# Who makes the low halves of the last four weight groups, and from which copy

## The reference

```python
x = x + layernorm(attn_ref(layernorm(x), ...))       # in_proj, conv, selective scan, gate, out_proj
x = x + layernorm(ffn_ref(layernorm(x), ...))

def ffn_ref(input, SU_ug, SU_dp, Wscale_ug, Wscale_dp, W_up, W_gate, W_down):
    x = fwht(x * SU_ug) / SCALE
    x_up = x @ W_up.T * (Wscale_ug[:INTER] * SCALE)
    x_gate = x @ W_gate.T * (Wscale_ug[INTER:] * SCALE)
    x = silu(x_gate) * x_up
    x = fwht(x * SU_dp) / SCALE
    return x @ W_down.T * (Wscale_dp * SCALE)
```

## Time and profile before

| | us |
|---|---|
| median of 3 runs | 2675.09 (2675.07 to 2676.07) |
| the profiled execution | 2677.31 |
| its span, first to last instruction | 2675.5 |
| PE busy | 2581.3 (96%) |
| DVE busy | 2238.6 (84%) |
| POOL busy | 2046.8 (77%) |
| ACT busy | 1818.1 (68%) |

### The profile page before, as it was taken

The page is one execution under the profiler, slowest core; times in us unless marked ns, Lnnn a source line. Parts: engine busy times, 40 slices in busy tenths (PEclk is TensorE's granted clock), DMA queues, the critical chain, the costliest instruction groups (busy, mean ns, idle before and its releaser), DMA issues.

```text
span 2675.5 us, 46296 instructions
## 1 busy us (share of the span) xinstructions
PE 2581.3 (96%) x16048; PEld 2190.1 (82%) x16048; DVE 2238.6 (84%) x2567; ACT 1818.1 (68%) x3939; POOL 2046.8 (77%) x1692
## 2 busy tenths in 40 slices
PE   7899889999999999999999999999999999989998
PEld 6566568989888898989888898988888898978887
DVE  6698799898889889898889889888889889989421
ACT  4576677777777767777777767777777767755322
POOL 6576778788797978888797988888797988777222
PEclk9999999999999999999999999999999999989999
DMA  5554245666666665766666665666666665656674
GB/s 179 193 185 151 105 164 199 232 214 219 227 217 218 217 228 198 242 211 228 228 213 217 216 227 204 237 210 235 217 219 219 212 220 205 228 177 233 259 269 164
DMA packets 165193, 564.41 MB, mean 211 GB/s; under 512 B 17248, under 2 KB 19680, under 8 KB 132960
## 3 DMA queue, kind: packets, MB, share of 16 engines
q1 hardware_dynamic: 164960, 561.44, 60.7%
HBM read 527.30 MB, written 34.08 MB: 210 GB/s over the span
## 4 chain that ended last, share of the span: by engine, by line
PE 77%; DVE 10%; ACT 8%; issue 3%; DMA 1%; POOL 1%; SPq 0%; POOLq 0%; DVEq 0%; ACTq 0%
PE pF L717 21%; PE hT L624 14%; PE pM L642 13%; PE pD L733 10%; PE pM L694 8%; DVE h L1147 5%; DVE acc L1160 3%; PE pD L754 3%; PE pM L664 3%; PE decay L717 2%; ACT decay L968 1%; PE hT L616 1%; PE pF L754 1%; ACT delta L945 1%; ACT delta L940 1%
## 5 line engine op out<-in xcount | busy, mean ns | idle before, releaser
L1147 DVE TENSOR_TENSOR_SCAN h<-decay,dbx 128x512 f32<-128x512 f32 x1024 | 1200.7, 1206 | 97.8 <-ACT decay L968 68.2
L1315 POOL TENSOR_TENSOR dbx<-u,bb 128x2048 f32<-128x2048 f32 (+1 forms) x272 | 1179.1, 4336 | 37.7 <-DVE h L1147 35.7
L968 ACT ACTIVATE decay<-delta,a_neg 128x255 f32<-128x255 f32 x2048 | 875.5, 468 | 310.0 <-DVE h L1147 302.6
L1160 DVE SCALAR_TENSOR_TENSOR acc<-hT,bcT,acc 128x1024 f32<-128x1024 f32 x480 | 609.3, 1269 | 127.7 <-PE hT L624 124.3
L717 PE MATMUL pF<-fxT_hi,wug 128*128 128x256 f32 x3632 | 710.2, 289 | 0.4 <-issue 0.4
L624 PEld LDWEIGHTS hT<-ident,h 128*128 128x128 f32 x4096 | 472.8, 141 | 148.5 <-issue 96.7
L717 PEld LDWEIGHTS pF<-fxT_hi,wug 128*128 128x128 f32 x3632 | 583.6, 192 | 0.9 <-issue 0.8
L624 PE MATMUL hT<-ident,h 128*128 128x128 f32 x4096 | 535.2, 274 | 33.6 <-DVE acc L1160 22.5
L717 PE MATMUL pF<-fxT_lo,wug 128*128 128x256 f32 x1816 | 514.8, 283 | 0.0
L642 PE MATMUL pM<-xnT,w_in 128*128 128x256 f32 x2016 | 480.9, 382 | 10.4 <-ACT hid L888 4.7
L642 PEld LDWEIGHTS pM<-xnT,w_in 128*128 128x128 f32 x2016 | 367.2, 192 | 55.8 <-ACT hid L888 6.3
(11 more groups left out here) (166 smaller groups left out, 2788.9 us busy)
## 6 DMA issues: line engine op xcount, KB each, us to landing
wug<-scratch_ug SPq DMA_DIRECT2D x243, 1024.0 KB, 4.8
wd<-scratch_wd SPq DMA_DIRECT2D x243, 512.0 KB, 4.0
w_in<-in_W_in SPq DMA_DIRECT2D x252, 256.0 KB, 2.9
bb<-scratch_bc SPq DMA_DIRECT2D x128, 256.0 KB, 4.7
xb<-in_hidden_states SPq DMA_DIRECT2D x16, 512.0 KB, 5.0
xr<-in_hidden_states SPq DMA_DIRECT2D x16, 512.0 KB, 5.9
out<-xr SPq DMA_DIRECT2D x16, 512.0 KB, 3.5
kept_ug<-scratch_ug SPq DMA_DIRECT2D x7, 1024.0 KB, 7.6
```

Source lines behind the costliest of these rows:

```text
L968: e = act.activation(da[q % 2][:, i, 1:], delta[c % 2][:, dt, 1:], ACT.Exp, scale=a_neg[:, dt, n:n + 1])
L1147: dve.tensor_tensor_scan(row(h[n % 2][:, tiles, :]), row(da[q % 2][:, :, :]), row(dbx[n % 2][:, tiles, :]), 0.0, ALU.mult, ALU.add).then_i ...
L1160: dve.scalar_tensor_tensor(acc[c % 2][:, tb, :], hT[:, :], cn, acc[c % 2][:, tb, :], ALU.mult, ALU.add).then_inc(acc_done, 1)
L1315: pool.tensor_tensor(dbx[n % 2][:, tiles, :], u[:, tiles, :], rows, ALU.mult).then_inc(done if restarts(c) else prod_done, 1)
```

## The change

For tiles 32 to 47 ScalarE reads the bank twice: after the high half it writes the same scaled tile again, unrounded, to one of two rows of `xr[1]`, which holds nothing else at that time. POOL, which makes no use of PSUM here, subtracts the high half from that copy and so makes the low half; VectorE no longer touches these tiles. TensorE now waits for the copy (`had_raw`) before it uses a bank again. POOL's 16 subtractions stand behind its `dbx` product of the even slot two or three after the one where ACT evacuates. Tiles 0 to 31 stay as they were.

```diff
+        FIRST_R = KT * SETS.index("r")
+        def raw_row(o):
+            return xr[1][:, o % 2, :].rearrange("p (a m) -> p a m", a=KT)
 # TensorE, had()
-                    if o >= len(had_bank):
-                        pe.wait_ge(had_lo, o - len(had_bank) + 1)
+                    old = o - len(had_bank)
+                    if old >= FIRST_R:
+                        pe.wait_ge(had_raw, old - FIRST_R + 1)
+                    elif old >= 0:
+                        pe.wait_ge(had_lo, old + 1)
 # ScalarE, had_high()
                 act.activation(split_row("hi", o), bank_tiles(o), ACT.Copy, scale=had_scale(o)).then_inc(had_hi, 1)
+                if o >= FIRST_R:
+                    if o == FIRST_R:
+                        act.wait_ge(had_stored["y_lo"], 16 * SETS.count("y"))
+                    if o >= FIRST_R + 2:
+                        act.wait_ge(had_lo, o - 1)
+                    act.activation(raw_row(o), bank_tiles(o), ACT.Copy, scale=had_scale(o)).then_inc(had_raw, 1)
 # VectorE, slot()
                 for o in HAD_EVAC.get((c, k), ()):
-                    had_low(o)
+                    if o < FIRST_R:
+                        had_low(o)
 # GpSimd
+            def had_low(o):
+                g, r = divmod(o, KT)
+                pool.wait_ge(had_raw, o - FIRST_R + 1)
+                if o == FIRST_R:
+                    pool.wait_ge(had_lo, FIRST_R)
+                if r == 0 and split_use(g):
+                    pool.wait_ge(had_stored[f"{SETS[g]}_lo"], 16 * split_use(g))
+                pool.tensor_tensor(split_row("lo", o), raw_row(o), split_row("hi", o).bitcast(F32), ALU.subtract).then_inc(had_lo, 1)
 # GpSimd, slot(), even slots, behind first_product(cur, 1) or b_times_u(cur, n)
+                for back_by in (3, 2):
+                    for o in HAD_EVAC.get(divmod(SLOTS * c + k - back_by, SLOTS), ()):
+                        if o >= FIRST_R:
+                            had_low(o)
```

More of the change, by code:

```diff
@@ L168, in fused_block @@
         had_setup = sem("had_setup"); w_first_in = sem("w_first_in"); diag_done = sem("diag_done"); turned_dve = sem("turned_dve"); turned_pool = sem("turned_pool")
-        had_mm = sem("had_mm"); had_hi = sem("had_hi"); had_lo = sem("had_lo")
+        had_mm = sem("had_mm"); had_hi = sem("had_hi"); had_lo = sem("had_lo"); had_raw = sem("had_raw")
         had_stored = {name: sem(f"had_stored_{name}") for name in split}
```

## The result

| | kernel before | changed kernel |
|---|---|---|
| median of five runs | 2675.09 us (2674.74 to 2677.32) | 2686.56 us (2685.01 to 2690.67) |
| profiled execution | 2677.31 us, span 2675.5 | 2687.23 us, span 2685.4 |
| TensorE's granted clock, mean | 0.993 | 0.991 |

The ratio is 1.0043, with a 95% interval of 1.0031 to 1.0054: slower by 11.5 us. Forecast were 2685.5 us and a range of 2679 to 2691.

The account below looks back on a forecast made before the run. TensorE was taken as the bound, with time lost in pass 1 or 2 not made up later. Copies 4.6 + tile 47 4.9 + clock 0.9 - 0 = 10.4 us on 2675.1 gave 2685.5 us, range 2679 to 2691.

Parts of the forecast that it names:

- DVE, 0 (0.5 at best): Pass 1: 16 remainders, 11.9 us, leave DVE but gain 0; at best 0.5 us, from tile 47 in slot 30.
- The copies, 4.6: Pass 1: ACT's copies delay evacuations TensorE waits for, eight times 0.58, 4.6 us; bounds 2.7 to 5.5.
- the eight places: Slots 4, 6, 8, 18, 20, 24, 26 and 28 of pass 1, where each copy makes TensorE 0.58 us later.
- The eighth, slot 8: Pass 1: 0.58 us lost like the others; at best a later store cuts TensorE's 2.23 us wait to 0.63, -1.6.
- POOL, hidden: Pass 1: 16 subtractions of 1.28 us, 20.5 us more on POOL, hidden by its lead over DVE: 0.
- The tight pairs: Slot pairs n=6 to 8 on POOL: 10.6 us of work against 9.9, falling back 2 in all, within a 4.9 us lead.
- The 3.1 us: Time of one POOL subtraction if contention with two-SBUF-input VectorE instructions held against scans too; 1.28 was expected.
- Tile 47, 4.9: Start of pass 2: POOL's late subtraction delays SP's store and the `wug` load; TensorE stands 4.9 us, bounds 4.4 to 6.0.
- The clock, 0.9 (0 or 1.7): Behind the new wait of about 5 us, TensorE's clock may drop: 0 or 1.7 us, middle 0.9 taken.
- Half hidden: Rival: the copies fall into other waits, or the weight load has more cover; 4.6 or 4.9 us remain, 2680; chance 0.15.
- DVE's relief: Rival: remainders delay sums in pass 1, so 3.3 us of TensorE's waits go, faster, 2671.8; chance 0.06.
- POOL as the bound: Rival: subtractions take 3.1 us each and `dbx` ends DVE's waits in pass 1; 2690, or some 2693; chance 0.09.

Follow-up runs that it names:

- number 6: Kernel before, with DVE making only a quarter of each low half for tiles 36 to 47, the rest left out: 2674.72 us against 2675.4.
- number 3: Changed kernel with ACT's copies moved behind the pM evacuations and tile 47's subtraction moved early on POOL: 2676.68 us, ratio 1.0002.
- number 5: Kernel before plus the sixteen ACT copies, read by nobody; DVE still makes the remainders, POOL does nothing new: 2679.88 us against 2675.4.
- number 1: Changed kernel with POOL's subtraction of tile 47 moved ahead of the first product of pass 2: 2680.32 us, ratio 1.0020.
- number 8: Changed kernel with POOL making each subtraction of tiles 32 to 46 twice: 2686.5 us, ratio 1.0044.
- number 7: Kernel of number 3 with POOL making each subtraction of tiles 32 to 46 twice: 2687.2 us, ratio 1.0046.
- number 2: Changed kernel with ACT's copies moved to the end of the next slot, behind the pM evacuation: 2682.9 us, ratio 1.0031.
- number 4: Kernel before with the change made for tile 47 alone, tiles 32 to 46 staying on DVE: 2682.22 us, ratio 1.0027.
- number 10: Changed kernel with ACT's pM evacuation first in each slot and tile 47's subtraction early on POOL: 2666.25 us against 2674.84.

## Why the prediction was right

**DVE, 0 (0.5 at best).** Held. Number 6 gives 0.7 us within an interval that holds zero. The one place I named, tile 47 between two sums in slot 30, gave 0.65 us in the traces, and the first products of pass 2 on POOL take it back, as I said. In the changed kernel the wait for `wug` covers that, but number 3 has no such wait, and its clock stayed at 1.00 there. It is 3.48 us ahead at the end of pass 1, 4.13 at the start of pass 2 and 3.25 at the first `pF` matmul, behind this new wait:

```profile
387.81 1.09 PE L630 MATMUL hT<-ident,h 128*128 128x128 f32 x8 [0.66 <-DVE fxT_lo L1194]
```

DVE is late there because its scan waited 1.57 us for `dbx` (0.86 in the kernel before). Number 6 gives its 0.40 us back at the same place.

**The copies, 4.6.** Held. The ledger has 4.1, at seven of the eight places, with 0.57 to 0.60 at each; number 5 has 4.5, and number 1 has 5.3 with the offload around it. The eighth, slot 8, cost nothing. I had given it 0.58 and bounded it at -1.6. My low end of 2.7 for the whole term doesn't follow from that: 4.6 less 1.6 is 3.0, which would have put the low end of the forecast's own range at 2682.0 instead of 2681.7. And not every wait of TensorE for ACT in the pass was for `pM`, as I wrote: one of 1.2 us was for `xnT`, before and after alike.

**POOL, hidden.** Held, and with more room than I counted. By the straight line one subtraction was to take 1.28 us; it took 1.27, all sixteen. The tight pairs would have fallen back by 2 us of a lead of 4.9; number 8 shows that of 19 us more at most some 1.4 reach TensorE, and none by the medians. With the work doubled the lead holds only as long as the copies come early, which number 7 shows and I hadn't seen. The Trainium skill (GPSIMD Engine Reference, Key points) names contention with VectorE instructions that have two SBUF inputs. DVE's scans and sums take one input from PSUM, they ran beside fourteen of the sixteen, and all sixteen took 1.27 to 1.28 us, so the trace agrees with the page as it stands. The 3.1 us came from my carrying its rule over to scans, against which it doesn't hold here. The long form is seen in the front part, beside a subtraction of DVE with both inputs in SBUF.

**Tile 47, 4.9.** Held. The wait took 5.2 us of time (10.12 less 4.93), or 4.5 counted from the end of pass 1, which leaves out the 0.65 that would have been lost anyway. Each link is as forecast: the subtraction behind the first product, the store right behind it, 4.25 us to the load (4.67 before), 4.78 to its landing. The row shows only 3.44 us of wait, since TensorE was itself late by the lower clock from 393 to 399; that part of the clock's loss cost nothing.

**The clock, 0.9 (0 or 1.7).** The mechanism was right and the size was not. Behind the wait the `pF` block ran at the lower level and took 2.3 us more, 2.6 with the transposes behind it, above my upper bound of 1.7, which came from a stretch that was only partly at that level. The Trainium skill (TensorE: Matmul & The Clock Gate, HAM oscillation) has the array restart at the low level behind a long wait; the changed kernel and number 2 agree (5.29 and 5.14 us for the block, a clock of 0.50 from 405 to 408 and from 399 to 405). Numbers 4 and 8, with the longest waits of all (4.28 and 4.20), agree only in part: the first matmuls ran at full speed and the clock fell after that (in number 4 0.28 us for an early one, 0.41 for the later ones), so that the price there was 1.5. The two kernels with the higher price had a drop of the clock in the 10 us ahead of the wait as well (0.55 from 393 to 396 in the changed kernel), the other two had none; whether that is the reason was not tested. Medians say the same of the whole term: 7.2 us for tile 47 alone, of which, by its ledger, 4.5 are the wait (TensorE 1.30 us ahead before it and 3.22 behind at `pF`) and 1.5 the clock; the remaining 1.2 is within the interval.

**The sum.** 10.4 was forecast and 11.5 measured. By the ledger the change itself makes 11.2: 4.1 for the copies, 4.5 for the wait, 2.6 for the clock behind it. Two of my three terms were within 0.5 us, and the clock's was 1.7 too small. By the medians the parts are 4.5 and 7.2, 11.7 together; by the other way round, taking each away from the changed kernel, 6.2 for tile 47's place (number 1) and 3.7 for the copies' (number 2), 9.9 together, as number 3 has it. The difference of some 2 us between the two ways is no more than the intervals allow. The drops of the clock in pass 1 are not to be explained by the change. The changed kernel and number 5 lost 1.7 us from 276 to 282; numbers 1 and 8, with the same copies in the same places, show 1.00 there. Why it falls in the one and not in the other stays open. With one profile of each kernel it can't be told whether such a drop belongs to the kernel or to the one execution.

**The rivals.** Half hidden fell: both halves were measured. DVE's relief fell with number 6, and with numbers 3 and 10, which have all of it and gain nothing that can be told. POOL as the bound fell with number 8, though number 7 is that very case: it needs the copies late and the work doubled.

## What to carry to other kernels

Before work is moved to an engine "with room", read what stands behind the place where it lands. Sixteen copies cost 4.5 us in front of the evacuation that TensorE waits for and nothing that can be told behind it. Moving that evacuation up gained 10.7 us by the medians with no work moved at all, of which the traces show 6.1 where the order was changed. Look for one instruction that a store and a load hang on: here 1.27 us of work, put behind a product in another engine's list, cost 7.2. And a relieved engine gives back only what somebody waited for: 4.8 us less work on DVE gave 0.7 by the medians, which can't be told from nothing, and 11.9 less, in numbers 3 and 10, no gain that can be told either.

## What the hardware showed that I had not expected

- The lower clock comes in where it hurts: the block right behind a wait of 3.4 to 3.6 us took 5.1 to 5.3 us instead of 3.0 in two kernels, and 4.5 behind waits of 4.20 and 4.28 in two others. The longer wait was not the dearer one.
- Elsewhere, drops of some 1.7 us each come, go and move between kernels with nearly the same work: from 292 to 302 us the granted clock was 0.83 in both kernels and in numbers 1 and 5, and 1.00 in numbers 2, 3, 4, 6 and 8. Numbers 2, 4, 6 and 8 had their drop at 313 instead (0.50 to 0.64 from 313 to 316), and only number 3 had none in the pass. Runs of one kernel spread over 3.6 to 8.2 us, so that the ends of one pair of executions tell little; a ledger does, if each drop is written down apart.
- POOL's subtraction of 128x512 didn't vary (1267 to 1282 ns) though DVE ran scans or sums beside it in fourteen of the sixteen places.
